# A four-layer fused kernel: own tiles for two mixes, five banks, and three context pieces and a weight moved behind the first steps of the recurrences

## The reference, cut to what matters

```python
xxx = xn + sx * maa_x
m = tanh(xxx @ maa_w1) @ maa_w2            # five mixes, rank 32 each
x_j = xn + sx * (maa_stack[j] + m[j])      # j: k=0, w=1, v=2, r=3, g=4
w = exp(-exp(time_decay + tanh(x_w @ decay_w1) @ decay_w2))
r, k, v, g = x_r @ Wr.T, x_k @ Wk.T, x_v @ Wv.T, silu(x_g @ Wg.T)
for t in range(T):                          # heads of size 16
    y_t = r_t @ (u * k_t^T v_t + state)
    state = k_t^T v_t + w_t * state
x = x + (groupnorm(y) * g) @ Wo.T
```

## Time and profile before

| what | us |
|---|---|
| median of 3 runs | 3271.57 (3270.77 to 3275.1) |
| the profiled execution | 3268.62 |
| its span, first to last instruction | 3267.3 |
| PE, DVE, ACT, POOL busy | 3079.5, 1357.2, 1117.7, 1006.7 |
| first stretch, first recurrence (rows below) | to 96.4, 96.4 to 243.6 |
| second stretch, second recurrence | to 321.15, from there to about 470 |

### The profile page before, as it was taken

The page is one execution under the profiler, slowest core; times in us unless marked ns, Lnnn a source line. Parts: engine busy times, 40 slices in busy tenths (PEclk is TensorE's granted clock), DMA queues, the critical chain, the costliest instruction groups (busy, mean ns, idle before and its releaser), DMA issues.

```text
span 3267.3 us, 43817 instructions
## 1 busy us (share of the span) xinstructions
PE 3079.5 (94%) x16648; PEld 2567.6 (79%) x16648; DVE 1357.2 (42%) x3056; ACT 1117.7 (34%) x2492; POOL 1006.7 (31%) x938
## 2 busy tenths in 40 slices
PE   6999888999999999999999999999899999989988
PEld 3555556898988888888889889988788877767876
DVE  5785876433333333433333333333311265653133
ACT  2333335333222233322232232223333455543331
POOL 4564554222122122222131131122254133335410
PEclk8898898999999999999999999999999999989999
DMA  6554641432112121121121121221011111101132
GB/s 217 183 174 167 192 137 55 143 130 105 57 70 87 67 90 70 70 80 66 72 99 58 70 103 58 89 83 52 32 65 52 56 43 43 43 28 68 52 95 80
DMA packets 95095, 285.93 MB, mean 88 GB/s; under 512 B 8280, under 2 KB 52824, under 8 KB 86056
## 3 DMA queue, kind: packets, MB, share of 16 engines
q1 hardware_dynamic: 94408, 282.44, 25.2%
q10 hardware_dynamic: 480, 0.69, 0.1%
HBM read 260.94 MB, written 22.15 MB: 87 GB/s over the span
## 4 chain that ended last, share of the span: by engine, by line
PE 76%; DVE 6%; POOL 6%; ACT 5%; issue 4%; DMA 3%; SPq 0%; POOLq 0%; ACTq 0%; DVEq 0%
PE bank L179 21%; PE bank L180 20%; PE bank L181 20%; PE bank L1789 5%; POOL W_lo L219 3%; PE bank L1774 2%; PE bank L2362 2%; ACT W_hi L210 2%; DMA W_raw<-in_weights 2%; PE bank L633 1%; DVE max L1982 1%; ACT prob L1871 1%; PE bank L2376 1%; POOL y L1213 1%; PE bank L581 1%
## 5 line engine op out<-in xcount | busy, mean ns | idle before, releaser
L2063 POOL TENSOR_SCALAR prob<-prob,inverse 112x376 f32<-112x376 f32 x256 | 143.9, 580 | 1285.6 <-DVE inverse L1988 1285.6
L219 POOL TENSOR_TENSOR W_lo<-W_raw,W_hi 128x1024 fp32r<-128x1024 f32 x138 | 329.8, 2411 | 155.5 <-ACT W_hi L210 153.5
L179 PE MATMUL bank<-ctx_hi,W_hi 128*128 128x376 f32 x1024 | 352.6, 344 | 4.4 <-DVE K_lo L261 2.8
L261 DVE SCALAR_TENSOR_TENSOR K_lo<-bank,vectors,K_hi 128x375 fp32r<-128x375 f32 (+1 forms) x288 | 172.9, 607 | 408.7 <-ACT K_hi L252 408.7
L180 PE MATMUL bank<-ctx_lo,W_hi 128*128 128x376 f32 x1024 | 342.6, 335 | 0.0
L181 PE MATMUL bank<-ctx_hi,W_lo 128*128 128x376 f32 x1024 | 342.0, 334 | 0.0
L179 PE MATMUL bank<-act_hi,W_hi 128*128 128x448 f32 x800 | 319.3, 399 | 10.9 <-DVEq L338 5.6
L180 PE MATMUL bank<-act_lo,W_hi 128*128 128x448 f32 x800 | 298.7, 373 | 0.0
L181 PE MATMUL bank<-act_hi,W_lo 128*128 128x448 f32 x800 | 298.2, 373 | 0.0
L1935 DVE TENSOR_TENSOR V<-bank,bv 128x512 f32<-128x512 f32 x168 | 116.2, 692 | 437.2 <-PE bank L1789 236.2
L1871 ACT ACTIVATE prob<-bank,minus 112x376 f32<-112x376 f32 x256 | 144.1, 576 | 433.4 <-DVE minus L1985 433.4
(11 more groups left out here) (256 smaller groups left out, 6378.9 us busy)
## 6 DMA issues: line engine op xcount, KB each, us to landing
W_raw<-in_weights SPq DMA_DIRECT2D x69, 1024.0 KB, 4.9
ctx_hi<-ctx_split SPq DMA_DIRECT2D x64, 752.0 KB, 4.3
ctx_lo<-ctx_split SPq DMA_DIRECT2D x64, 752.0 KB, 5.8
v_spread<-v_rows SPq DMA_DIRECT2D x128, 224.0 KB
att<-in_ctxT SPq DMA_DIRECT2D x16, 376.0 KB, 5.2
ctx_split<-W_hi SPq DMA_DIRECT2D x16, 376.0 KB, 3.8
ctx_split<-W_lo SPq DMA_DIRECT2D x16, 376.0 KB, 4.8
W_hi<-ctx_split SPq DMA_DIRECT2D x32, 188.0 KB, 4.1
```

The lines of the kernel that those rows point to most:

```text
L179: nc.tensor.matmul(dst, left[0], right[0], start=first, stop=False)
L219: pool.tensor_tensor(k.Wl[:, slot, cs, :], k.Wraw[:, cs, :], k.Wh[:, slot, cs, :].bitcast(F32), ALU.subtract).then_inc(*k.w_low.now((n, i)))
L261: dve.scalar_tensor_tensor(out=low, in0=src, scalar=bias, in1=high.bitcast(F32), op0=ALU.add, op1=ALU.subtract).then_inc(*k.banks.draining ...
L2063: pool.tensor_scalar(k.Pm[:, h, :], k.Pm[:, h, :], k.rsum[:, h:h + 1], 1.0, ALU.mult, ALU.mult).then_inc(*k.prob_done.now((n, h)))
```

## The change

Mix 2 and then mix 1 get tiles of their own (slot 2, `xh2` and `xl2`, in the space of `rT`, `state` and `tmp`); mix 0 keeps slot 0 and mix 3 slot 1. The stretch rotates over five banks, 0, 1, 6, 2 and 5. PE makes mixes 0 and 1 between the v projections, the outputs of the first half before the decays, k's first output between the chunks of mix 3, and r's last. ACT and DVE are ordered to match. Waits are added where a new use of banks 2 and 5 or of the shared space could meet an old one. `W_VALUES[0]` (the weight v1_0) is split at step 3 of the first recurrence; the first recurrence's g and o are split at 11 and 16 instead of 9 and 14, and g is loaded at step 5. In the second half k comes before r; pieces 13 to 15 of the context are split at steps 1 to 8, and the first chunks are loaded back at step 10 instead of 6.

```diff
-ORDER = (["v", "k", "r", "v1_0", "g", "o", "v", "r", "k"] + ...
+ORDER = (["v", "k", "r", "v1_0", "g", "o", "v", "k", "r"] + ...
-SLOT = ([0, 1, 0, 2, 1, 0, 1, 1, 0] + ...
+SLOT = ([1, 0, 1, 2, 0, 1, 0, 0, 1] + ...
-MIX_SLOT = {2: 0, 0: 0, 1: 1, 3: 1, 4: 0}
+MIX_SLOT = {2: 2, 0: 0, 1: 2, 3: 1, 4: 0}
+MIX_BANKS = (0, 1, 6, 2, 5)
+SPLIT_AT = [{"v1": 3, "g": 11, "o": 16}, {"g": 9, "o": 14}]
+CX_LATE = {1: 13, 4: 14, 7: 15}
...
 def pe_rwkv(k):
...
         for c in range(C):
+            if half and c == 3:
+                pe_centre(k, 0, C - 1)
+                pe.wait_ge(*k.scan_done[0, 63])
             pe_mix(k, half, 2, c)
         for o in range(C):
             for c in range(C):
                 pe_project(k, half, "v", o, c)
             if half and o == 0:
                 pe_variance(k, 0, C - 1)
+                pe.wait_ge(*k.outer_done[0, 63])
             if half and o == 1:
                 pe_spread_root(k, 0, C - 1)
-        for c in range(C):
-            pe_mix(k, half, 0, c)
+            for i in range(2):
+                pe_mix(k, half, o // 2, 2 * (o % 2) + i)
         if half:
             for i in range(HB):
                 pe_out_chunks(k, 0, i, range(C))
-        for c in range(C):
-            pe_mix(k, half, 1, c)
         pe_decay(k, half)
-        for c in range(C):
-            pe_mix(k, half, 3, c)
+        pe_mix(k, half, 3, 0)
+        pe_mix(k, half, 3, 1)
+        for c in range(C):
+            pe_project(k, half, "k", 0, c)
+        pe_mix(k, half, 3, 2)
+        pe_mix(k, half, 3, 3)
         pe_decay_out(k, half)
-        for name in "kr":
-            for c in range(C):
-                pe_project(k, half, name, 0, c)
+        for c in range(C):
+            pe_project(k, half, "r", 0, c)
...
 def x_slot_free(half, j):
-    return {0: ("v", half, C - 1), 3: ("dec1", half), 4: ("k", half, C - 1)}[j]
+    return {2: None, 1: ("v", half, C - 1), 4: ("k", half, C - 1)}[j]
...
 def act_rwkv(k):
...
-        act_split_weight(k, w["r"])
+        act_split_weight(k, w["k" if half else "r"])
         for c in range(C):
             act_mix(k, half, 1, c)
-        if half:
-            act_split_weight(k, w["k"])
...
-        for c in range(C):
-            act_mix(k, half, 3, c)
-        if half == 0:
-            act_split_weight(k, W_VALUES[0])
+        act_mix(k, half, 3, 0)
+        act_mix(k, half, 3, 1)
+        if half:
+            act_split_weight(k, w["r"])
+        act_mix(k, half, 3, 2)
+        act_mix(k, half, 3, 3)
...
+        act_projected(k, half, "k", 0)
         act_decay(k, half)
         act_decay_to_bank(k, half, 0)
-        act_projected(k, half, "k", 0)
...
 def pool_rwkv(k):
...
         if half:
+            pool_split_weight(k, w["k"])
             pool_cx(k, 8)
             pool_cx(k, 9)
         pool_split_weight(k, w["r"])
-        if half:
-            pool_cx(k, 10)
-            pool_cx(k, 11)
-            pool_split_weight(k, w["k"])
-        for m in range(12 if half else 4, 8 * half + 8):
+        for m in range(10 if half else 4, 13 if half else 8):
             pool_cx(k, m)
-        if half == 0:
-            pool_split_weight(k, W_VALUES[0])
...
+            if half and n in CX_LATE:
+                pool_cx_high(k, CX_LATE[n])
+            if half and n - 1 in CX_LATE:
+                pool_cx_low(k, CX_LATE[n - 1])
...
 def sp_rwkv(k):
...
             sp_cx_pass(k, 8, 10)
-            sp_load_weight(k, w["k"])
-            sp_cx_pass(k, 10, 14)
-        sp_load_weight(k, w["g"])
+            sp_load_weight(k, w["r"])
+            sp_cx_pass(k, 10, 13)
+            sp_load_weight(k, w["g"])
         for n in range(64):
             sp_spread(k, half, n + 4)
-            if half and n < 2:
-                sp_cx_store(k, 14 + n)
+            if half and n - 2 in CX_LATE:
+                sp_cx_pass(k, CX_LATE[n - 2], CX_LATE[n - 2] + 1)
+            if half == 0 and n == 5:
+                sp_load_weight(k, w["g"])
...
-            if n == 6:
+            if n == (10 if half else 6):
                 sp_first_chunks(k, half)
```

More of the change, by code:

```diff
@@ L60 @@
 MADE = 1
-ORDER = (["v", "k", "r", "v1_0", "g", "o", "v", "r", "k"] + [f"v1_{g}" for g in range(1, MADE)] + ["g", "o", "fr", "fk"]
+ORDER = (["v", "k", "r", "v1_0", "g", "o", "v", "k", "r"] + [f"v1_{g}" for g in range(1, MADE)] + ["g", "o", "fr", "fk"]
          + ["fv", "q1_0", "k1_0", "o1_0"] + [f"{w}1_{g}" for g in range(1, G) for w in ("qko" if g < MADE else "qkvo")] + UNIQUE[UNIQUE.index("q2_0"):])
@@ L803, in act_mix @@
         act.wait_ge(*k.banks.filled(x_slot_free(half, j)))
+    if c == 0 and half and j == 2:
+        act.wait_ge(*k.y_done[0, 63])
     xh, _ = x_in_slot(k, MIX_SLOT[j], c)
@@ L820, in act_projected @@
     act.wait_ge(*k.banks.filled(key))
+    if (name, o) == ("r", 0):
+        act.wait_ge(*k.banks.filled(("dec1", half)))
     act.copy(flat({"k": k.kT, "r": k.rT}[name][:, o]), k.banks.tile(key)[:, 0:HALF]).then_inc(*k.banks.draining(key))
@@ L826, in act_keys_to_bank @@
     act.wait_ge(*k.banks.drained(("k", half, o)))
+    if o == 0:
+        act.wait_ge(*k.banks.drained(k.last_mixed[half, KEY_BANK]))
     if o or half:
@@ L834, in act_decay_to_bank @@
     act.wait_ge(*k.decay_done[half, o])
+    if o == 0:
+        act.wait_ge(*k.banks.drained(k.last_mixed[half, DECAY_BANK]))
     if o or half:
@@ L845, in act_init @@
         act.wait_ge(*k.y_done[half, n - 4])
-    elif half:
-        act.wait_ge(*k.y_done[half - 1, 60 + n])
+    else:
+        act.wait_ge(*k.banks.filled(("dec1", half)))
     b0 = half * HB
@@ L1018, in dve_mix_low @@
     xh, xl = x_in_slot(k, MIX_SLOT[j], c)
+    if c == 0 and half and j == 2:
+        dve.wait_ge(*k.y_done[0, 63])
     dve.wait_ge(*k.x5_high[half, j, c])
@@ L1036, in dve_outer @@
         dve.wait_ge(*k.y_done[half, n - 4])
-    elif half:
-        dve.wait_ge(*k.y_done[half - 1, 60 + n])
+    else:
+        dve.wait_ge(*k.banks.filled(("dec1", half)))
     if d == 0:
@@ L3216, in build @@
             shift_tiles(k, tiles(outer))
+            with ExitStack() as inner:
+                mix_tiles(k, tiles(inner))
             with ExitStack() as inner:
```

83 lines of the change are left out of this document (55 added, 28 removed).

## The result

The changed kernel is slower: 3288.05 us (median of 6 runs, 3282.46 to 3290.49) against 3273.01 for the kernel before in the same runs. The ratio is 1.0037, 95% interval 1.0026 to 1.0048, so 9 to 16 us slower. I had forecast 3264.1 and faster; the result lies outside my range. The profiled executions differ by more than the medians, 3289.23 against 3268.62.

A forecast was written before the change was run, and what follows sets the result against it. It took a PE, DVE and ACT chain to bound the first stretch and POOL's y, paced by DVE, the loop. Net gains of 2.4 and 5.1 us sum to 7.5: 3271.57 to 3264.1 us, range 3252 to 3275.

The forecast's parts named there:

- First stretch, item 1: v block before the first recurrence: first output ends at about 46 us, 0.7 us earlier, last v at 58.4 us.
- item 3: First stretch, from tanh at 69.7 us through mix 3, decays and r's copy: y 0 at 86, 10 us earlier.
- Second stretch: Before the second recurrence: tanh 9.5 us earlier; y 0 at 310.3, held by piece 12's split on POOL.
- First recurrence: Gives back part of the first stretch's 10 us through late spreads and o's split; net 2.4 us earlier.
- Second recurrence: Spread 4 used 7 us after issue, step 10 at 338.5; chunks at step 10 cost nothing extra; net 5.1 us earlier.
- Edits at no cost: Added waits, k and r swap, slots and output order cost nothing; a wait losing its cover would cost 1.94 us.
- A: Recurrences: DVE's light steps and spread waits absorb the moved work; gain 17 us, 3254.6 us; chance 0.22.
- B: Loop starts: spreads stand behind the whole queue, 2.9 us per extra MB; gain 4.6 or 3 us; chance 0.15.
- C: Stretches: first tanh only 3 us earlier, second gains 6 us, loops give it all back; 3271.6 us; chance 0.13.
- D: Recurrences: SP's holds make spread 15, then o, and spread 11 late; slower, 3279 us; chance 0.10.
- The rule against it: Ring order puts a spread behind all SP issued before: 2.9 and 8.5 us in the loops, gain 4.6 instead of 7.5.

The follow-up runs named there:

- the dense v: Changed kernel with one more wait: PE begins the v projections of either half only when mix 2's last chunk is complete; ratio to before 1.0044.
- the kernel with the loops alone: Kernel before with only the change's recurrence side (v1_0, g, o, pieces 13 to 15 and chunks at their new steps); ratio to before 1.0066.
- the one with g at step 5: Kernel before with g's 1 MB load issued at step 5 of the first recurrence instead of in front of it; ratio to before 1.0015.
- The stretches alone: Changed kernel with everything moved behind a y 0 put back (v1_0, g, o, pieces 13 to 15, chunks as before); ratio to before 1.0025.

## Why the prediction was wrong

The profile's +20.6 us against my -7.5 make 28.1 us. 4.0 of them lie behind the recurrences, in the scatter named above; the rest in these steps. In short, the stretches gave 12.3 us less than forecast, in the first half because PE's work was priced at 2.4 GHz. The recurrences cost 11.8 us more, and the two terms of it that the runs single out are o's split at step 16, taken at 1.5 us, and the chunks at step 10, taken at nothing.

**First stretch, item 1** (7.9 us, 5.0 of them here): "v's first output ends at about 46 us", and then three projections of 2.46 us and six mixes of 0.84. The order was right, but v's first output ended at 46.7, no earlier than before, and the durations were those of 2.4 GHz, taken from the stretch of the earlier trace rows in which PE is dense. With PE fed chunk by chunk, v's second output and the mixes ahead of it ran at 1.2 GHz: 12 x (0.375 - 0.205) + (3.35 - 1.77) = 3.6 us. The two turns of two mixes and a projection that ran at 2.4 GHz took 4.33 and 4.36 us instead of 4.14; with the 0.7 us of the first output this makes the 5.0. I had named low clock only for the decay outputs and r (2 us, not put into the sum), and it came there too: item 3's 16.3 us were 18.9. That item follows ACT alone and has ACT start r's copy straight behind its own work; it stood 2.18 us for PE.

**Second stretch** (4.4 us): the same block, at 0.50 of the clock from 267 to 275 us; the tanh is 5.4 us earlier instead of 9.5. That the low clock is the reason here is not shown: with the dense v it was back at 1.00 by 271 us, and the tanh still came 51.7 us behind the last y (51.9 changed). That y 0 would stand behind piece 12 on POOL and not behind r was right. That this queue order could be otherwise I did not ask; moved alone it took 5.3 us off the second half in the profile.

**First recurrence** (5.3 us): to outer 11 I had 24.3 us from y 0, and it was 24.6. This term was right: for the megabyte ahead of spread 11 I took 1.5 us more than before, it was 1.9, and the wait at spreads 10 and 11 is 7.4 us, inside my 5 to 9. It held because SP's stand behind v1_0's split had let the DMA engines run empty; without that stand the same load cost spread 10 5.4 us, which my range of nothing to 2.9 did not hold. "A cost between 0 and 4.72 - 3 x 0.5 = 3.2 us; I take 1.5" for o at step 16 was mis-sized: 4.8 us. The lead of three tiles gave POOL no slack here; the bound should have been the whole split. The other 1.7 us are spread over the steps and were not followed.

**Second recurrence** (6.5 us): spread 4 used 7.0 us after its issue was right to a tenth. To step 10 it took 30.6 us instead of 28.2. "I count the two as equal", for the chunks at step 10 against step 6, was wrong: at step 10 they stand ahead of o's load, and ACT holds the key copy behind o's split. y 10 to y 16 took 24.5 us, 20.9 before, and 2.1 to 3.5 of it went with o's load moved.

**Edits at no cost** stood: no wait shown in the traces belongs to the added ones on `scan_done`, `outer_done` or `y_done`.

Of the rivals, A (all absorbed) is refuted by the kernel with the loops alone and by the one with g at step 5. B's 2.9 us for a megabyte was met at neither place of the changed kernel (1.9 us at spread 11; spread 4 used after 7.0 and not 8.5 us), and was too small with g at 5 in the kernel before. C was right that the stretches would give less. D named the mechanism in the second recurrence, o late on ACT behind SP's hold, at 0.10, and sized it far too high: 8.8 + 4.7 us against some 3.5. The stretches alone, 12.3 us short, turn a forecast of -7.5 us into +4.8. The chance of slower, 0.12, came from counting each doubt alone, while the doubts leaned the same way: PE's durations and the slack of POOL were taken from rows of before in which nothing else stood in the way.

**The rule against it.** I took transfers to overlap. The Trainium skill, "DMA: Bandwidth & Descriptors", section on queues, rings and completion order, has a queue's descriptors consumed in ring order on each engine. The traces agree for what stands behind: spread 4 behind g's load (used 6.5 us after its issue with 4.89 us of wait, and back to no wait when the load goes behind it), and o behind the chunks (10.6 us from issue to use). It doesn't give the size: behind the same megabyte a spread came 1.6 to 5.4 us later, by what the engines had to do besides.
